# Third layer's remainders on GpSimd, seven-block one-hot batches of the pair stage on ScalarE, first layer's tail later in the step

## Chip, cores and metric

One core of one Trainium2 chip. The metric is the device time of one launch in microseconds, the slowest core's; here there is one. Engines: TensorE (PE), VectorE (DVE), ScalarE (ACT), GpSimd (POOL) and SyncE (SP, which only issues transfers). Lines as L777 are lines of the kernel before.

## What is computed

A graph of 6250 nodes with 64 features and 200000 random edges sorted by target goes through four layers, each with a residual and a layer norm:

```python
x = layernorm(x + sage(x))        # layer 1: mean over neighbours, two dense products (64->128->64), aggregated twice
x = layernorm(x + gcn(x))         # layer 2: 1/sqrt(deg) on both ends
x = layernorm(x + signed(x))      # layer 3
x = layernorm(x + attention(x))   # layer 4: softmax over the edges of a target

# layer 3
Wh  = h @ W + b;  Wr = Wh[row];  Wc = Wh[col]
sim = (Wr * Wc).sum(-1) / maximum(|Wr| * |Wc|, 1e-8)
base = adj_v * softplus(deg_coeff[0] * deg_v + deg_coeff[1]) * (row != col)
prop_pos = segment_sum(base *  relu( sim) * Wc, row)
prop_neg = segment_sum(base * -relu(-sim) * Wc, row)
out = scale * (coeff[0] * prop_pos + coeff[1] * prop_neg + coeff[2] * Wh)
```

## The kernel before

The nodes make 49 blocks of 128 (`NB`, `P`). The edges are grouped by pair of blocks: for source block i and target block j the slots of the pair hold up to 128 edges, one on each partition. Gathers and scatters become matmuls with one-hot matrices of 128x128 (slot against node within the block), built on the chip. Values for such matmuls are split in three bf16 parts (a value, its remainder, the remainder's remainder) so that they are exact enough.

The program is written by hand for each engine, with semaphores; each engine runs its instructions in the order in which they stand. It has a head (to about 190 us), the **pair stage** (to 1370), the second layer (to 1877), the **third layer** (to about 2900) and the fourth.

**Pair stage** (`pairs_*`, L473 to L840). A loop over `t`, each step in 13 sub-steps `n`, works on five blocks at once. For block j = t: edge records come in and are turned on TensorE (L582), VectorE marks the source blocks (L735), TensorE counts runs (offsets L593, `runs` L608 to L611), VectorE takes the ranks from them (`ranks`, L740). For j - 1: one-hots of ranks and fields on VectorE (L749, L754) and 108 slot matmuls on TensorE (L626), which put the edges in their slots (`E3`, L760, L763 and ScalarE's L555). For i = t - 3, all 49 pairs of a block: VectorE builds the one-hots of sources `OS` and targets `OD` in seven batches b of seven blocks (`hots`, L777, 14 instructions of 128x896); SP stores both for the later layers (L476, L477); TensorE multiplies `OS` with `OD` four blocks at a time into one of two PSUM buffers (`count`, L638), ScalarE evacuates (L542), and TensorE uses the counts against the node features (`use`, L651). The one-hots have three buffers (`NHB`); a batch waits for the count and the store of the batch three before. For d = t - 4 the first layer's dense part is run (`dense`): VectorE's sum and `cat` (L785 to L794), a transpose on TensorE (L663), two products (L666, L669) with ScalarE's evacuations between (L516, L521), ScalarE's `T` (L524, sub-step 9), VectorE's sum into `X` (L797, L800; sub-steps 9 and 10), a transpose of two rows of `E3` on TensorE (L674, L675; sub-step 10), and ScalarE's evacuation of it with two DMA issues (L529 to L532; sub-step 11).

**Third layer** (`pairs3_*`, L1108 to L1333). A loop over n, seven pairs (`G`) a step, 343 steps (`NG`). For step n + 4 the "columns" are built, one-hots of 128x1792 in place of loaded rows: every third step on ScalarE as Abs and Relu (L1211, L1213), else on VectorE (L1263). TensorE gathers both ends (L1171, L1178), ScalarE evacuates one (L1221), VectorE forms dot products (L1271, L1274, L1276) and after seven steps the coefficient of a block (L1282 to L1296). For step n - 8 the gathered rows are scaled: three blocks of seven (`KA`) on ScalarE (L1230), four on GpSimd (L1148). For n - 9 the first remainder is taken, three blocks on VectorE (`remainder`, L1300), four on GpSimd (L1153). For n - 10 GpSimd takes the second (L1158), and for n - 11 TensorE adds all up in the target block (`spread`, L1190). The values have four buffers.

Of the kernel before, what the change touches and what calls it, by code (L numbers as in the profile page):

```python
# [53 lines left out]
def gnn_kernel(nc, x, src, dst, eattr, ew, ew2, W1n, b1n, W1r, Wl1, bl1, W2n, b2n, W2r, Wl2, bl2,  # L54
               W2g, b2g, dcoef, cpar, spar, W3, watt, bias3, out):
    with ExitStack() as ctx:
# [256 lines left out]
        def head_dve(dve):  # L313
# [177 lines left out]
        def pairs_act(act):  # L491
# [14 lines left out]
            def dense(i, n):  # L506
# [18 lines left out]
                elif n == 11:  # L525
# [49 lines left out]
        def pairs_pe(pe):  # L575
# [79 lines left out]
            def dense(i, n):  # L655
# [14 lines left out]
                elif n == 10:  # L670
                    pe.wait_ge(t_out.at, i + 1)
# [35 lines left out]
        def pairs_dve(dve):  # L707
# [58 lines left out]
            def hots(i, n):  # L766
# [9 lines left out]
                for o_, s in ((OS, 0), (OD, 1)) if n == 0 else (((OS, 0),) if n % 2 else ((OD, 1),)):  # L776
                    ins = dve.tensor_tensor(o_[r].rearrange("p c (r k) -> p c r k", k=2), bc(r1v.unsqueeze(1), [P, 7, D, 2]),  # L777
                                            bc(sdb[i % 2][:, s, 7 * b:7 * b + 7, :].unsqueeze(2), [P, 7, D, 2]), ALU.is_equal)
                    (dv if s == 0 else hot8).by(ins)
# [426 lines left out]
        def pairs3_act(act):  # L1206
            def columns(n):
                if n % 3 == 0:
# [4 lines left out]
                    hot_a.by(act.activation(rw[r], rw[r], ACT.Relu, bias=1.0, scale=-1.0))  # L1213
# [44 lines left out]
        def pairs3_dve(dve):  # L1258
            def columns(n):
                if n % 3:  # L1260
# [17 lines left out]
            def coefficient(j):  # L1278
# [1027 lines left out]
```

## Time and profile before

| | us |
|---|---|
| median of 3 runs | 3884.51 (3882.99 to 3885.42) |
| profiled run | 3884.62 |
| its span, first to last instruction | 3882.9 |

| engine | busy us of the span | share |
|---|---|---|
| VectorE | 3187.8 | 82% |
| TensorE matmul | 3024.9 | 78% |
| ScalarE | 2164.4 | 56% |
| GpSimd | 1348.8 | 35% |

These shares are means over stages with different limits, so they say little alone; the stages are read one by one from busy times in a stretch of the span, then from the waits in it and from one step in order of time. A row of the order of time has start, length, engine, line and what is written from what; "x3" merges three instructions in a row, and the bracket is the idle time of the engine before it and what ended it. The clock granted to TensorE was 0.924 of its full speed on the mean.

### The profile page before, as it was taken

What the parts mean: (1) busy time and instruction counts of PE and PEld (TensorE: products, weight loads), DVE (VectorE), ACT (ScalarE), POOL (GpSimd) and SP (SyncE); (2) the same over time, 40 slices, a digit from 0 to 9 for tenths busy, and PEclk for the clock granted to TensorE, in tenths of its full rate; (3) what the DMA queues carried; (4) which work ended last, traced back from release to release, by engine and by line L of the source; (5) the groups of instructions that cost most, each with busy time, mean ns of one, the idle gap of its engine ahead of it and who ended that gap; (6) DMA issues with size and microseconds to landing.
All of it is one profiled execution on the core that took longest, in us unless ns stands there. A gap on an engine that the chain in (4) does not pass through costs nothing.

```text
span 3882.9 us, 125317 instructions
## 1 busy us (share of the span) xinstructions
PE 3024.9 (78%) x50473; PEld 2698.4 (69%) x50473; DVE 3187.8 (82%) x6939; ACT 2164.4 (56%) x5734; POOL 1348.8 (35%) x1644
## 2 busy tenths in 40 slices
PE   0288888888888869899777777777765888778876
PEld 0167777777777669899677777677755777777775
DVE  7599999999999823233799999999976889888886
ACT  5323333333333410001688788788765888888887
POOL 2000000000000000000487787787772555555554
PEclk9999999999999989999899999999986888888887
DMA  8156666666666779889677677677746888888884
GB/s 212 55 166 209 207 206 209 207 207 209 209 208 208 241 293 369 338 330 328 214 244 235 222 243 232 225 247 232 229 140 219 272 259 263 265 269 261 262 259 146
DMA packets 655937, 907.64 MB, mean 234 GB/s; under 512 B 363977, under 2 KB 587882, under 8 KB 636411
## 3 DMA queue, kind: packets, MB, share of 16 engines
q1 hardware_dynamic: 633240, 800.64, 64.1%
q10 hardware_dynamic: 19763, 94.38, 6.4%
q8 instruction: 406, 6.65, 0.7%
q0 software_dynamic: 2352, 4.52, 0.6%
q14 instruction: 176, 1.44, 0.1%
HBM read 651.96 MB, written 247.40 MB: 232 GB/s over the span
## 4 chain that ended last, share of the span: by engine, by line
DVE 38%; PE 32%; DMA 11%; ACT 9%; issue 8%; SPq 2%; POOL 1%; ACTq 0%; DVEq 0%; POOLq 0%
PE ps L626 8%; PE ps L964 7%; DVE U L754 5%; DMA U<-AD 3%; DMA A<-ROWS 3%; DVE EDG L777 3%; DMA T<-ROWS 3%; DVE U L1271 3%; DVE EDG L1300 3%; DVE U L1263 2%; PE ps L1178 2%; PE ps L1190 2%; PE ps L1171 2%; DVE U L1634 2%; SPq L1398 2%
## 5 line engine op out<-in xcount | busy, mean ns | idle before, releaser
L542 ACT ACTIVATE U<-ps 128x512 bf16<-128x512 f32 (+1 forms) x637 | 359.1, 573 | 666.1 <-PE ps L638 665.9
L1148 POOL TENSOR_TENSOR EDG<-U,edge 128x256 f32<-128x256 f32 x343 | 244.0, 711 | 850.8 <-DVE edge L1296 732.4
L1466 ACT ACTIVATE U<-U,T 128x65 f32<-128x65 f32 x1806 | 459.9, 340 | 86.0 <-PE ps L1554 81.4
L1178 PE MATMUL ps<-U 128*128 128x65 bf16 x7203 | 300.1, 198 | 217.7 <-DVE edge L1274 215.0
L487 POOL DMA_INDIRECT U<-REC,nod x49 | 48.8, 996 | 1160.7 <-PE ps L582 1038.5
L964 PE MATMUL ps<-U 128*128 128x192 bf16 x4802 | 416.5, 247 | 38.4 <-DVE U L1041 19.3
L964 PEld LDWEIGHTS ps<-U 128*128 128x128 bf16 x4802 | 401.6, 98 | 46.8 <-DMA U<-AD 24.2
L1178 PEld LDWEIGHTS ps<-U 128*128 128x128 bf16 x7203 | 261.2, 101 | 241.3 <-DVE edge L1274 237.4
L777 DVE TENSOR_TENSOR EDG<-edge,EDG 128x896 bf16<-128x896 bf16 x686 | 408.3, 621 | 10.0 <-DMA OSD<-EDG 9.0
L1492 POOL TENSOR_TENSOR U<-U 128x455 f32<-128x455 f32 x258 | 276.2, 1071 | 305.6 <-DVE U L1634 305.6
L651 PE MATMUL ps<-EDG,U 128*128 128x193 bf16 x2401 | 312.8, 252 | 62.0 <-ACT U L542 40.4
L626 PE MATMUL ps<-U 128*128 128x98 bf16 (+1 forms) x5292 | 341.9, 223 | 0.3 <-DVE U L754 0.3
L1158 POOL TENSOR_TENSOR EDG<-EDG 128x448 f32<-128x448 f32 x343 | 329.3, 960 | 25.0 <-DVE EDG L1300 25.0
L626 PEld LDWEIGHTS ps<-U 128*128 128x128 bf16 x5292 | 328.3, 98 | 5.3 <-DVE U L754 0.8
L1171 PE MATMUL ps<-U 128*128 128x65 bf16 x7203 | 298.7, 197 | 13.3 <-ACT U L1213 7.7
L754 DVE TENSOR_TENSOR U<-U 128x882 bf16<-128x882 bf16 x528 | 295.8, 616 | 0.0
L1171 PEld LDWEIGHTS ps<-U 128*128 128x128 bf16 x7203 | 280.8, 100 | 20.1 <-issue 12.6
L1230 ACT ACTIVATE EDG<-U,edge 128x64 f32<-128x64 f32 x1029 | 279.6, 338 | 19.1 <-DVE edge L1296 10.4
L1046 DVE TENSOR_REDUCE A<-ps 128x64 f32<-128x192 f32 x98 | 34.3, 355 | 293.8 <-PE ps L964 293.6
L651 PEld LDWEIGHTS ps<-EDG,U 128*128 128x128 bf16 x2401 | 181.4, 99 | 131.7 <-ACT U L542 120.1
L638 PE MATMUL ps<-EDG 128*128 128x128 bf16 x2401 | 245.6, 222 | 30.8 <-DVE EDG L777 30.8
L1221 ACT ACTIVATE U<-ps 128x455 f32<-128x455 f32 x343 | 185.1, 540 | 148.6 <-PE ps L1171 146.4
(302 smaller groups left out, 7328.1 us busy)
## 6 DMA issues: line engine op xcount, KB each, us to landing
U<-AD SPq DMA_DIRECT2D x98, 1568.0 KB, 8.7
U<-ROWS SPq DMA_DIRECT2D x343, 448.0 KB, 4.4
OND<-EDG SPq DMA_DIRECT2D x343, 224.0 KB
OSD<-EDG SPq DMA_DIRECT2D x343, 224.0 KB
AD<-U ACTq DMA_DIRECT2D x49, 1568.0 KB, 6.4
EDG<-ROWS SPq DMA_DIRECT2D x343, 224.0 KB, 5.1
U<-OND SPq DMA_DIRECT2D x303, 224.0 KB, 5.3
EDG<-OSD SPq DMA_DIRECT2D x189, 224.0 KB, 4.6
```

The costliest lines, as they stand in the source:

```text
L542: ev4.by(act.activation(prow[i % NPW][:, P * g:P * (g + m)], ps[4 + gg % 2][:, 0:P * m], ACT.Copy))
L626: ins = pe.matmul(ps[3][:, o:o + NB * (f1 - f0)], w_, FR[h][:, c, f0:f1, :, k], start=(h + c + k + f0 == 0), stop=(last and f0 == 0))
L651: ins = pe.matmul(ps[6][:, 0:XW], prow[i % NPW][:, P * j:P * j + P], Xs[:, j, :], start=(j == 0), stop=(j == NB - 1))
L754: ins = dve.tensor_tensor(FR[h][:, :, f, :, :], OH[j % 2][:, HC * h:HC * h + HC, :, :], bc(L_[j % NL][:, 2 + f, HC * h:HC * h + HC, :].uns ...
L777: ins = dve.tensor_tensor(o_[r].rearrange("p c (r k) -> p c r k", k=2), bc(r1v.unsqueeze(1), [P, 7, D, 2]), bc(sdb[i % 2][:, s, 7 * b:7 * ...
L964: ins = pe.matmul(ps[q][:, 0:192], arow[r][:, P * j:P * j + P], (XsB if p else XsA)[:, j, :, :].rearrange("p s f -> p (s f)"), start=(j == ...
L1158: low3.by(pool.tensor_tensor(V3[m % 4][:, 2, :, :], V3[m % 4][:, 1, :, :], S3[m % 4][:, 1, :, :], ALU.subtract))
L1171: ins = pe.matmul(ps[h][:, 65 * k:65 * k + 65], rw[r][:, 2 * P * k + P:2 * P * k + 2 * P], Ws[:, i0 + k, s_, 0:65], start=(s_ == 0), stop= ...
L1178: ins = pe.matmul(ps[2 + h][:, 65 * k:65 * k + 65], rw[r][:, 2 * P * k:2 * P * k + P], Ws[:, j, s_, 0:65], start=(s_ == 0), stop=(s_ == 2))
L1230: ins = act.activation(V3[m % 4][:, 0, k, :], Wc[:, j % 2, i0 + k, 0:D], ACT.Copy, scale=edge[:, 6 + j % 2, i0 + k:i0 + k + 1])
L1466: ins = act.activation(V4[k % NV][:, 0, c, :], H[d % 3][:, s, :], ACT.Copy, scale=a4[d % 2][:, s:s + 1])
L1492: look.by(pool.tensor_tensor(V4[k % NV][:, 2, :, :], V4[k % NV][:, 1, :, :], S4[k % NV][:, 1, :, :], ALU.subtract))
```

## The change

1. Third layer: the first remainder of all seven blocks is GpSimd's, which waits for ScalarE's copies; VectorE's `remainder` is gone. `KA` is 5 instead of 3, so ScalarE scales five blocks and GpSimd two. ScalarE builds the columns of every fifth step instead of every third, VectorE the others. The coefficient is one instruction shorter, from a constant `sc[:, 19:20]` made in the head.
2. Pair stage: the targets' one-hots `OD` of batches 2 and 5 are made by ScalarE (`hots` in `pairs_act`), as Abs of a difference per block and one Relu per batch, spread over sub-steps 0 to 4 and 5 to 9; SP and TensorE wait for them on a semaphore of their own. There are four buffers instead of three, the fourth in `U`.
3. First layer's tail: VectorE's two sums go from sub-steps 9 and 10 to 11 and 12, TensorE's row transposes from 10 to 12 (and no longer wait for `T`), ScalarE's evacuation of them from 11 to 12.

The diff, cut to its core:

```diff
-        NHB = 3
+        NHB = 4
+        BYA = (2, 5)
...
 def pairs_sp
                 sp.wait_ge(hot8.at, k + 1)
+                if b in BYA:
+                    sp.wait_ge(hot_a.at, hot_a.o + made_a(k))
...
 def pairs_act, dense
-                elif n == 11:
+                elif n == 12:
                     act.wait_ge(row_t.at, i + 1)
...
+            def hots(i, n):
+                if n >= 5 * len(BYA):
+                    return
+                b = BYA[n // 5]
+                k = NH7 * i + b
+                r = k % NHB
+                if n % 5 == 0:
+                    act.wait_ge(slot_ev.at, i + 1)
+                    if k >= NHB:
+                        kk = k - NHB
+                        act.wait_ge(count4.at, NG4 * (kk // NH7) + (7 * (kk % NH7) + 6) // 4 + 1)
+                        act.wait_ge(hot_st[r].at, 32 * (k // NHB))
+                for c in ((0, 1), (2, 3), (4, 5), (6,), ())[n % 5]:
+                    ac.by(act.activation(OD[r][:, c, :], iota1, ACT.Abs, scale=-1.0, bias=E3[:, i, 1, 7 * b + c:7 * b + c + 1]))
+                if n % 5 == 4:
+                    act.wait_ge(ac.at, ac.n)
+                    hot_a.by(act.activation(OD[r].rearrange("p c r -> p (c r)"), OD[r].rearrange("p c r -> p (c r)"), ACT.Relu, bias=1.0, scale=-1.0))
...
                     if d is not None:
                         dense(d, n)
+                    if i is not None:
+                        hots(i, n)
...
 def pairs_pe
+                pe.wait_ge(hot_a.at, hot_a.o + made_a(NH7 * i + (g + m - 1) // 7))
...
-                elif n == 10:
-                    pe.wait_ge(t_out.at, i + 1)
+                elif n == 12:
                     pe.wait_ge(x_in.at, i + 1)
...
 def pairs_dve, dense
-                elif n == 9:
+                elif n == 11:
                     dve.wait_ge(t_out.at, i + 1)
...
-                elif n == 10:
+                elif n == 12:
                     dve.wait_ge(x_in.at, i + 1)
...
 third layer
-        KA = 3
+        KA = 5
...
-            return n // 3 + 1
+            return n // 5 + 1
...
                     pool.wait_ge(vm_p.at, m + 1)
-                    rem3p.by(pool.tensor_tensor(V3[m % 4][:, 1, KA:G, :], V3[m % 4][:, 0, KA:G, :], S3[m % 4][:, 0, KA:G, :], ALU.subtract))
+                    pool.wait_ge(vm_a.at, m + 1)
+                    rem3.by(pool.tensor_tensor(V3[m % 4][:, 1, :, :], V3[m % 4][:, 0, :, :], S3[m % 4][:, 0, :, :], ALU.subtract))
...
-                if n % 3 == 0:
+                if n % 5 == 0:
...
-                dvf.by(dve.tensor_scalar(a, b_, 0.0, sc[:, 16:17], ALU.max, ALU.mult))
-                dvf.by(dve.tensor_scalar(c_, b_, 0.0, sc[:, 17:18], ALU.min, ALU.mult))
+                dvf.by(dve.tensor_scalar(a, b_, 0.0, sc[:, 19:20], ALU.max, ALU.mult))
                 dve.wait_ge(dvf.at, dvf.n)
-                dvf.by(dve.tensor_tensor(a, a, c_, ALU.add))
+                dvf.by(dve.scalar_tensor_tensor(a, b_, sc[:, 17:18], a, ALU.mult, ALU.add))
```

VectorE in the pair stage around the sum into `X`, sub-steps 9 to 12, before (L777 is a one-hot batch):

```order
L754 TENSOR_TENSOR U<-U,EDG 128x9x98 x2
L797 TENSOR_TENSOR X<-X,ps 128x64 [waits t_out]
L777 TENSOR_TENSOR EDG<-edge,EDG 128x896 [waits hot_st2,pair_count,slot_evac]
L800 TENSOR_TENSOR X<-X,brow 128x64 [waits x_in]
L777 TENSOR_TENSOR EDG<-edge,EDG 128x896
```

and in the change, where the numbers of lines have moved (L815 is a batch of `OS`, L819 one of `OD`, L838 and L841 are L797 and L800):

```order
L792 TENSOR_TENSOR U<-U,EDG 128x9x98 x2
L815 TENSOR_TENSOR EDG<-edge,EDG 128x896 [waits hot_st0,pair_count,slot_evac]
L838 TENSOR_TENSOR X<-X,ps 128x64 [waits t_out]
L815 TENSOR_TENSOR EDG<-edge,EDG 128x896 [waits hot_st1,pair_count,slot_evac]
L841 TENSOR_TENSOR X<-X,brow 128x64 [waits x_in]
L819 TENSOR_TENSOR EDG<-edge,EDG 128x896
```

The sum stands one batch later, and the batch of `OD` between is gone.

ScalarE in the pair stage from sub-step 7 on, before (L542 evacuates counts, L521 the hidden layer, L504 the turned records, L524 writes `T`, L529 the rows):

```order
L521 ACTIVATE MISC<-ps,bias1s 128x128 [waits layer_out,hidden]
L504 ACTIVATE U<-ps 128x360 [waits field_hot,rec_turned]
L542 ACTIVATE U<-ps 128x512 [waits pair_count] x2
L524 ACTIVATE T<-ps 128x64 [waits layer_out]
L542 ACTIVATE U<-ps 128x512 [waits pair_count] x2
L529 ACTIVATE EDG<-ps 49x256 [waits rw_st0,rows_t]
L531 DMA ROWS<-EDG 49x256 [waits rows_ev]
L532 DMA ROWS<-EDG 49x2x128
```

and in the change (L578 Abs, L581 Relu, L559 evacuation, L538, L521, L541, L546 for L521, L504, L524, L529):

```order
L538 ACTIVATE MISC<-ps,bias1s 128x128 [waits layer_out,hidden]
L578 ACTIVATE EDG<-edge,E 128x128 x2
L521 ACTIVATE U<-ps 128x360 [waits field_hot,rec_turned]
L559 ACTIVATE U<-ps 128x512 [waits pair_count]
L578 ACTIVATE EDG<-edge,E 128x128
L559 ACTIVATE U<-ps 128x512 [waits pair_count]
L541 ACTIVATE T<-ps 128x64 [waits layer_out]
L581 ACTIVATE EDG<-EDG 128x896 [waits act_step]
L559 ACTIVATE U<-ps 128x512 [waits pair_count] x3
L546 ACTIVATE EDG<-ps 49x256 [waits rw_st0,rows_t]
L548 DMA ROWS<-EDG 49x256 [waits rows_ev]
L549 DMA ROWS<-EDG 49x2x128
```

Three Abs and a Relu stand between the evacuations, and the row evacuation with its two issues comes after one more evacuation of counts.

VectorE in the third layer, one step, before:

```order
L1271 TENSOR_TENSOR U<-ps,U 128x448 [waits r_got,c_ev]
L1274 TENSOR_TENSOR edge<-ps,U 128x7 [waits coef]
L1276 TENSOR_REDUCE edge<-U 128x7 [waits fast_step]
L1263 TENSOR_SCALAR U<-U,iotap 128x1792 [waits rows_ld4]
L1300 TENSOR_TENSOR EDG<-EDG 128x192 [waits value_act]
```

and GpSimd's and VectorE's work in the change (GpSimd's is L1185 for L1148, L1191 for L1153, L1195 for L1158):

```order
L1185 TENSOR_TENSOR EDG<-U,edge 128x128 [waits spread,coef]
L1191 TENSOR_TENSOR EDG<-EDG 128x448 [waits value_act,value_pool]
L1195 TENSOR_TENSOR EDG<-EDG 128x448 [waits layer_out]
...
L1308 TENSOR_TENSOR U<-ps,U 128x448 [waits r_got,c_ev]
L1311 TENSOR_TENSOR edge<-ps,U 128x7 [waits coef]
L1313 TENSOR_REDUCE edge<-U 128x7 [waits fast_step]
L1300 TENSOR_SCALAR U<-U,iotap 128x1792 [waits rows_ld4]
```

VectorE has no operation on the values any more, and GpSimd's remainder of all 448 columns waits for ScalarE's copies.

## Rows read from the trace of the kernel before

**Rows 1.** Busy time by stretch: pair stage and third layer.

```profile
core 0: us, PE busy (x) PEld busy (x) DVE busy (x) ACT busy (x) POOL busy (x), PEclk, DMA share, GB/s
300.00:1300.00 1000.00, 885.85 (x11893) 717.51 (x11891) 971.12 (x1963) 362.70 (x873) 35.68 (x39) 1.00 0.67 209
1900.00:2800.00 900.00, 686.95 (x15045) 648.70 (x15041) 860.65 (x1882) 725.02 (x1515) 703.59 (x915) 0.94 0.72 236
```

**Rows 2.** Waits, 200 to 1300 us: total us, times, longest us.

```profile
DVE X L797 <- ACT T L524: 27.9, 44, 0.7
```

**Rows 3.** One step in order of time: start us, us, engine, line [idle <-releaser].

```profile
1004.81 0.34 PE L611 MATMUL ps<-EDG,identb 18*128 18x98 bf16 x4
...
1005.75 1.13 DVE L740 TENSOR_REDUCE EDG<-ps 128x10 bf16<-128x490 f32 x2
...
1005.89 0.41 PE L638 MATMUL ps<-EDG 128*128 128x128 bf16 x4 [0.40 <-DVE EDG L777]
...
1008.15 0.33 PE L663 MATMUL ps<-ident,MISC 128*128 128x128 f32 x1 [0.66 <-DVE MISC L794]
...
1016.54 0.36 ACT L521 ACTIVATE MISC<-ps,bias1s 128x128 f32<-128x128 f32 x1
...
1016.79 0.47 ACT L504 ACTIVATE U<-ps 128x360 bf16<-128x360 bf16 x1
...
1017.80 0.28 PEld L651 LDWEIGHTS ps<-EDG,U 128*128 128x128 bf16 x4 [0.28 <-ACT U L542]
...
1018.48 0.22 DVE L797 TENSOR_TENSOR X<-X,ps 128x64 f32<-128x64 f32 x1 [0.63 <-ACT T L524]
1018.62 0.62 DVE L777 TENSOR_TENSOR EDG<-edge,EDG 128x896 bf16<-128x896 bf16 x1
...
1019.29 1.69 DVE L777 TENSOR_TENSOR EDG<-edge,EDG 128x896 bf16<-128x896 bf16 x3
...
1023.14 0.36 ACT L529 ACTIVATE EDG<-ps 49x256 bf16<-49x256 f32 x1
...
1024.23 1.08 ACT L542 ACTIVATE U<-ps 128x512 bf16<-128x512 f32 x2 [0.72 <-PE ps L638]
...
1026.00 1.10 PE L593 MATMUL ps<-U,after 128*18 128x49 bf16 x36
...
1029.71 0.66 DVE L740 TENSOR_REDUCE EDG<-ps 128x10 bf16<-128x490 f32 x1
```

**Rows 4.** Groups by line, VectorE, third layer: xcount | busy us, mean ns | idle.

```profile
L1300 DVE TENSOR_TENSOR EDG<-EDG 128x192 f32<-128x192 f32 x305 | 192.3, 631 | 18.7 <-ACT EDG L1230 17.9
...
L1263 DVE TENSOR_SCALAR U<-U,iotap 128x1792 bf16<-128x1792 bf16 x204 | 177.2, 869 | 0.0
```

**Rows 5.** The same of ScalarE.

```profile
L1230 ACT ACTIVATE EDG<-U,edge 128x64 f32<-128x64 f32 x918 | 249.5, 338 | 5.5 <-DVE edge L1296 5.3
L1211 ACT ACTIVATE U<-U,negp 128x1792 bf16<-128x1792 bf16 x102 | 181.3, 1777 | 0.0
L1213 ACT ACTIVATE U<-U 128x1792 bf16<-128x1792 bf16 x102 | 173.1, 1697 | 3.2
L1221 ACT ACTIVATE U<-ps 128x455 f32<-128x455 f32 x306 | 165.3, 540 | 134.5 <-PE ps L1171 132.5 <-POOL EDG L1148 0.9
```

**Rows 6.** Single lines, third layer: duration ns min/median/max.

```profile
L1148 POOL TENSOR_TENSOR EDG<-U,edge x305: 605/638/1109, 1900.0 to 2799.4; 128x256 f32<-128x256 f32 x153
...
L1158 POOL TENSOR_TENSOR EDG<-EDG x305: 924/928/1365, 1899.1 to 2798.5; 128x448 f32<-128x448 f32 x153
...
L1263 DVE TENSOR_SCALAR U<-U,iotap x204: 676/741/1392, 1900.1 to 2796.7; 128x1792 bf16<-128x1792 bf16 x102
...
L1300 DVE TENSOR_TENSOR EDG<-EDG x305: 344/702/1102, 1901.7 to 2797.3; 128x192 f32<-128x192 f32 x153
```

**Rows 7.** In order of time, third layer, VectorE beside GpSimd.

```profile
2309.97 0.61 POOL L1148 TENSOR_TENSOR EDG<-U,edge 128x256 f32<-128x256 f32 x1
...
2310.32 0.75 DVE L1263 TENSOR_SCALAR U<-U,iotap 128x1792 bf16<-128x1792 bf16 x1
```

More of the change, by code:

```diff
@@ L434, in gnn_kernel @@
         Xs3 = Xs[:, :, 0:3 * D].rearrange("p b (s f) -> p b s f", s=3)
-        NHB = 3
+        NHB = 4
         NH7, GH = 7, 7 * P
-        OS = [EDG[:, 4730 + 448 * i:4730 + 448 * i + 448].bitcast(BF16).rearrange("p (c r) -> p c r", r=P) for i in range(NHB)]
-        OD = [EDG[:, 6074 + 448 * i:6074 + 448 * i + 448].bitcast(BF16).rearrange("p (c r) -> p c r", r=P) for i in range(NHB)]
+        spare = part(o2 + 6272, 896)
+        OS = [o.bitcast(BF16).rearrange("p (c r) -> p c r", r=P)
+              for o in [EDG[:, 4730 + 448 * i:4730 + 448 * i + 448] for i in range(NHB - 1)] + [spare[:, 0:448]]]
+        OD = [o.bitcast(BF16).rearrange("p (c r) -> p c r", r=P)
+              for o in [EDG[:, 6074 + 448 * i:6074 + 448 * i + 448] for i in range(NHB - 1)] + [spare[:, 448:896]]]
+        BYA = (2, 5)
         rst = [EDG[:, 7802 + P * i:7802 + P * i + P].bitcast(BF16) for i in range(2)]
@@ L466, in gnn_kernel, with made_a @@
         hot_st = [sem(f"hot_st{i}") for i in range(NHB)]
+        def made_a(k):
+            return len(BYA) * (k // NH7) + sum(b <= k % NH7 for b in BYA)
         def at_step(t):
@@ L775, in hots @@
                         dve.wait_ge(hot_st[r].at, 32 * (k // NHB))
[L776 to L779, printed above, removed]
+                if n % 2 or n == 0:
+                    ins = dve.tensor_tensor(OS[r].rearrange("p c (r k) -> p c r k", k=2), bc(r1v.unsqueeze(1), [P, 7, D, 2]),
+                                            bc(sdb[i % 2][:, 0, 7 * b:7 * b + 7, :].unsqueeze(2), [P, 7, D, 2]), ALU.is_equal)
+                    (hot8 if b in BYA else dv).by(ins)
+                if n % 2 == 0 and b not in BYA:
+                    hot8.by(dve.tensor_tensor(OD[r].rearrange("p c (r k) -> p c r k", k=2), bc(r1v.unsqueeze(1), [P, 7, D, 2]),
+                                              bc(sdb[i % 2][:, 1, 7 * b:7 * b + 7, :].unsqueeze(2), [P, 7, D, 2]), ALU.is_equal))
             def dense(i, n):
@@ L1212, in columns @@
                     act.wait_ge(ac.at, ac.n)
-                    hot_a.by(act.activation(rw[r], rw[r], ACT.Relu, bias=1.0, scale=-1.0))
+                    hot_ea.by(act.activation(rw[r], rw[r], ACT.Relu, bias=1.0, scale=-1.0))
             def ends(n):
@@ L1296, in coefficient @@
                 coef.by(dve.tensor_tensor(d_, a, E3v[:, :, j, 2], ALU.mult))
-            def remainder(m):
-                dve.wait_ge(vm_a.at, m + 1)
-                rem3.by(dve.tensor_tensor(V3[m % 4][:, 1, 0:KA, :], V3[m % 4][:, 0, 0:KA, :], S3[m % 4][:, 0, 0:KA, :], ALU.subtract))
             for n in range(4):
@@ L1304, in pairs3_dve @@
             for n in range(NLAST):
-                if 0 <= n - 9 < NG:
-                    remainder(n - 9)
                 if n < NG:
@@ L1713, in gnn_kernel @@
         z_inc, z_carry, z_fix, z_agg, z_read = again(ln_i), again(ln_o), again(normed), again(pj_t), again(pj_ev)
-        z_cat, z_t, z_ct, z_h, z_r, z_o, z_x2 = again(pj_mm), again(pj_out), again(nr_i), again(nr_o), again(ws_i), again(ws_o), again(hot_a)
+        z_cat, z_t, z_ct, z_h, z_r, z_o, z_x2 = again(pj_mm), again(pj_out), again(nr_i), again(nr_o), again(ws_i), again(ws_o), again(hot_ea)
         z_tab, z_tabst = again(hot_d), again(c_got)
```

18 lines of the change are left out of this document (10 added, 8 removed).

## Prediction

> **What bounds the kernel now.** I read first the busy time by stretch, because the page's shares mix stages. In the pair stage (300 to 1300 us taken) VectorE is busy 97.1% of the time and TensorE 88.6%; ScalarE has only 36%. In the third layer (1900 to 2800 us taken) VectorE is busy 95.6%, ScalarE 80.6%, GpSimd 78.2%, TensorE 76.3% [rows 1]. So VectorE is the engine to relieve in both, and the change does that. What matters is who is second.
>
> The waits of the pair stage come next [rows 2]. VectorE waits for one thing, `T` from ScalarE, 0.63 us a step. Then I read one step in order of time [rows 3]: TensorE in turn waits there for VectorE, 0.40 us for a one-hot batch and 0.66 for `cat` (L794), so the two hold each other. It lasts 1029.71 - 1005.75 = 23.96 us from one start of L740 to the next. TensorE's last run-count matmuls (L611) end at 1004.81 + 0.34 = 1005.15; VectorE starts the ranks that need them (L740) only at 1005.75, so it is late there by about 0.5. From that start, ranks, fields and `cat` take 2.35 us, and TensorE, which waited for `cat`, goes on at 1008.15. From 1008.15 to the next 1005.15 + 23.96 TensorE never again waits for VectorE, only for ScalarE. **This is the number that decides the pair stage**: VectorE can give back about 0.5 us a step before TensorE's own loop, which runs through ScalarE's evacuations, sets the pace.
>
> In the third layer a step of seven blocks lasts 900 / 305 = 2.95 us [rows 1, 4] (305 is the count of L1300 in that stretch). By the same division VectorE is busy 2.82 us of it, ScalarE 2.38, GpSimd 2.31, TensorE 2.25. VectorE has no room here, and its remainder (L1300) has a mean of 631 ns where its minimum is 344 [rows 4, 6].
>
> **Pair stage, part by part.**
> - VectorE loses two of fourteen one-hots. Three in a row take 1.69 where one takes 0.62 [rows 3], so one costs 0.535 from start to start: 2 x 0.535 = 1.07 us a step. Its wait of 0.63 for `T` would be a further gain if it vanished.
> - TensorE's gain. With VectorE early, the ranks start just behind the run counts, 1005.23 for 1005.75, and `cat` comes 0.52 us earlier. **-0.52**. Without `cat` TensorE would be there at 1008.15 - 0.66 = 1007.49; two Abs ahead of an evacuation (0.54, below) put that later and the 0.40 of waiting for a one-hot batch, which goes, earlier: 1007.63, just when `cat` is there. So the whole 0.52 stands.
> - ScalarE's additions. Seven Abs of 128x128 and a Relu of 128x896 per batch, in pieces between the evacuations (the second order listing). A 128x128 activation with its bias from a tile takes 0.36, and the next starts 0.25 after it (1016.54, 1016.79) [rows 3]; for a source in SBUF I add 0.02, an estimate, and take 0.27. Where TensorE has much else to do these are hidden: before the first count group ScalarE sits idle, and after the third there are 5 us of run counts and slot matmuls. They show at one place, sub-step 7 to 9: between the copy of the records (L504, 1016.79) and what stands ahead of it (L521, 1016.54) two Abs are put, ahead of the evacuation for which TensorE already waits (0.28 us at 1017.80). **+0.55**, up to 0.8 if an Abs takes its full 0.36 and more. The Relu at sub-step 9 lies beside the 3.4 us of slot matmuls.
> - The tail moved later. The row transposes and ScalarE's row evacuation with two DMA issues stood at sub-steps 10 and 11, now both at 12. Today the row evacuation starts at 1023.14 and the next count evacuation 1.09 us later, at 1024.23, and TensorE waits for it [rows 3]. In the new order the transposes come behind one more count and one more use group, so the evacuation starts at about 1023.9, the same 1.09 us then delay the next group (1024.99 + 0.60), and only the last two use groups (0.6 us) follow: the next step starts at about 1026.25 for 1026.00. **+0.25**.
> - VectorE's wait for `T` does not go. Today VectorE is there at 1018.48 - 0.63 = 1017.85. It comes there 0.52 earlier with its whole step, and batch 5's second one-hot (-0.54) is gone while its first now stands ahead (+0.54): 1017.33. `T` comes 0.52 earlier and three Abs later (+0.8): 1018.76. It waits about 1.45 us. It then still reaches the next ranks some 0.4 us before TensorE has ended the run counts, so the longer wait costs nothing.
> - The fourth buffer and the stores: SP now waits for ScalarE's mark at batches 2 and 5, and batch 6 and the next step's queue behind it. ScalarE's marks fall at sub-steps 4 and 9, as VectorE's did; the buffer is wanted again four batches later, over 6 us. I take nothing.
>
> Sum: -0.52 + 0.55 + 0.25 = +0.28 us in each of 48 full steps: **+13 us**. Ends: -0.52 alone if both additions hide (-25 us), and no gain at `cat` with +0.85 (+41 us).
>
> **Third layer, part by part**, per step of 2.95 us [rows 1, 4 to 6].
> - VectorE: the remainder goes, 0.631 less 0.085 of overlap = -0.55. Columns rise from 2/3 to 4/5 of the steps, 0.133 x (0.869 - 0.085) = +0.10. The coefficient has one small operation less in seven steps, -0.03 (the head has one more, once: nothing). New 2.34; if every column operation is held by GpSimd for another 0.15, 2.46.
> - GpSimd: scaling two blocks instead of four. The minima for 256 and 448 columns are 0.605 and 0.924, 1.66 ns a column, so -0.21; the remainder grows from 256 to 448 columns, +0.32. New 2.31 + 0.11 = 2.42. It no longer waits for VectorE's part (L1158) but for ScalarE's scaled copies.
> - ScalarE [rows 5]: two more copies, 2 x (0.338 - 0.10) = +0.48; columns fall from 1/3 to 1/5 of the steps, 0.133 x (1.777 + 1.697) = -0.46. New 2.40.
> - TensorE unchanged, about 2.25 with its short waits in it.
>
> So the bound falls from 2.82 to about 2.42, and three engines then lie within 0.1 of each other. Today the step is 1.045 of its busiest engine. With ScalarE's block of 3.5 us every fifth step, and waits in both directions between three full engines, I take 1.10: 2.67 us, **-0.28 us a step**. The steps with values are 343 - 9 = 334: **-94 us**. Ends: 2.52 (1.045 of 2.42), -144 us; and 2.85, -33 us, if the queues (four value buffers, two of PSUM) don't ride over the blocks.
>
> **A rule against it.** In the trace VectorE and GpSimd hold each other up: the column operation that starts at 2310.32 beside GpSimd's of 2309.97 (to 2310.58) takes 0.75 where the minimum is 0.676, and GpSimd's three operations (L1153 has the shape of L1148) have minima of 0.605 + 0.605 + 0.924 = 2.13, but are busy 2.31 [rows 1, 6, 7]. If all such operations exclude each other for their whole length, a step has 2.13 of GpSimd, 0.667 x 0.68 of columns and 0.34 of remainder: 2.93, nearly today's 2.95. After the change it would be 2.24 + 0.8 x 0.68 = 2.78, scaled by 2.95 / 2.93 to 2.80: -0.15 x 334 = -50 us. Against it: the column operation above was delayed by 0.07, though GpSimd's had 0.26 to go.
> The Trainium skill ("SBUF — State Buffer", section "Who interferes with whom") states it so: the shared port pair is held for the whole instruction and the loser fully blocks. By that the third layer gives 50 us rather than 94; the traced pair of operations speaks for a shorter hold.
>
> **The rivals.**
> 1. VectorE stays the bound of the pair stage: 1.07 + 0.63 = 1.70 us x 48 = -82, with -94 gives 3709 us. For it speaks its 97%; against it the 0.5 us of room above. 8%.
> 2. Whole-length exclusion between VectorE and GpSimd, as above: 3884.6 + 13 - 50 = 3848 us. 17%.
> 3. Slower: GpSimd's remainder waits for ScalarE's block. Between the last copies before a block and the next lie 3.47 of columns, 0.54 of evacuation and 0.34 + 4 x 0.24 of five copies, 5.3 us, against 2.42 of GpSimd's own work: 2.9 us per five steps, 0.58 a step, 3.00 in all, +0.05 x 334 = +17, and with the pair stage 3915 us. It decides this way if ScalarE enters a block with no lead over GpSimd; with 2.9 us of lead it costs nothing. Against it: VectorE's remainder has the same wait today and sits 17.9 us in it over 305 steps [rows 4], with blocks every third step. 7%.
>
> **Numbers.** The profiled run took 3884.6 us, 1.7 more than its span, and the median of three is 3884.5, so the sum needs no shift. Forecast: 3884.6 + 13 - 94 = **3804 us**, 62%. The remaining 6% are things not seen, split evenly. The range is 3742 to 3874: the ends of both stages taken together would be 3716 and 3893, and the range leaves out rival 1, rival 3 and the outermost of these. A measurement can tell 0.2%, about 8 us. Faster by more: 0.86; within: 0.07; slower: 0.07.
>
> **What would show it.** Pair stage: a step of 24.0 to 24.4 us, VectorE's busy share down to about 92% with a wait for ScalarE's `T` of 1 to 2 us a step and a new short wait for the run counts, ScalarE near 60%. A step under 23.4 us would break the argument on TensorE's loop. Third layer: steps of 2.5 to 2.85 us, GpSimd over 85% busy, VectorE under 92%. The column operation's mean above 0.95 us with GpSimd's operations stretched speaks for rival 2; GpSimd's 128x448 remainder waiting over 150 us for ScalarE's copies speaks for rival 3. The second and fourth layers should not move.

## The result, and the profile after

| | median, us | ratio to before, 95% interval |
|---|---|---|
| before | 3883.51 (3871.6 to 3887.23, 10 runs) | |
| changed | 3893.5 (3886.1 to 3910.43, 10 runs) | 1.0039 [1.0027, 1.0051] |

The changed kernel is slower by 0.4%, 10 us, where 3804 us and a gain of 2% were forecast; the time lies outside the range. The profiled run of the changed kernel took 3910.43 us and is the slowest of its ten, so the two traces differ by more (span 3908.7 for 3882.9, +25.8) than the medians do: what is read below from one trace is larger than what the ten executions have on the median. Ratios, here and below, are to the kernel before as it was measured together with the changed one.

Busy time in the stretches of [rows 1], same columns; the changed kernel:

```profile
300.00:1300.00 1000.00, 866.22 (x11437) 706.06 (x11435) 893.69 (x1803) 572.77 (x1482) 91.64 (x39) 0.96 0.63 201
1900.00:2800.00 900.00, 695.27 (x15232) 657.06 (x15233) 841.44 (x1613) 737.18 (x2024) 725.04 (x898) 0.92 0.74 241
```

VectorE has fallen from 97.1% to 89.4% in the pair stage, as meant, but PEclk from 1.00 to 0.96. In the third layer VectorE is still at 93.5% (95.6% before).

The third layer's first product in each of its steps marks that stage. Before, then changed (duration ns min/median/max, first and last start):

```profile
L1271 DVE TENSOR_TENSOR U<-ps,U x343: 609/611/625, 1881.2 to 2877.6; 128x448 f32<-128x448 f32 x172
```
```profile
L1308 DVE TENSOR_TENSOR U<-ps,U x343: 609/612/626, 1921.8 to 2893.0; 128x448 f32<-128x448 f32 x172
```

So of the 25.8 us the stages up to the third layer lost 40.6, the third layer gave back 996.4 - 971.2 = 25.2 (94 were forecast), and what lies behind it was 10.4 longer. Nothing is changed there, and it is scatter between executions: from the last of these products to the end it takes 998 to 1016 us in the 14 traces of this case. The third layer scatters too: with it as before it takes 992 to 996 us in four traces (this first one, `pair_alone`, `tail_alone` and `hots_alone`), and with part 1 962 to 974 in seven, so its gain is known to be 18 to 35 us and no closer.

**Pair stage.** I took the step from one start of VectorE's sum into `X` (L838 now, L797 before) to the next. Before, all of the 43 full steps (the last five are shorter) take 23.95 to 24.00 us. Now 30 take 24.1 to 24.4 (forecast: 24.24), and 13, every third or so, take 26.2 to 26.7. 13 x 2.06 = 27 us for these (26.42 for 24.36) and 43 x 0.34 = 15 for the normal growth give 42, and 40.6 of it are left where the third layer begins. The waits from 300 to 1300 us, of VectorE for `T` and for the run counts, to be held against [rows 2], and of TensorE for ScalarE's count evacuation (total us, times, longest us):

```profile
DVE X L838 <- ACT T L541: 68.1, 40, 2.5
DVE EDG L778 <- PE ps L649: 35.5, 40, 2.0
```
```profile
PE ps L690 <- ACT U L559: 103.8, 148, 1.6
```

1.70 us a step for `T` and the new wait for run counts (L649) are what was foretold. A long step from inside, in order of time and then by stretch (columns of [rows 1]), changed kernel:

```profile
1000.69 0.38 ACT L546 ACTIVATE EDG<-ps 49x256 bf16<-49x256 f32 x1
...
1001.40 0.57 ACTq L549 DMA_DIRECT2D ROWS<-EDG  x1
...
1002.01 0.77 ACT L559 ACTIVATE U<-ps 128x512 bf16<-128x512 f32 x2 [0.95 <-PE ps L677]
...
1002.67 0.60 PE L690 MATMUL ps<-EDG,U 128*128 128x193 bf16 x5 [1.32 <-ACT U L559]
...
1004.69 0.59 PE L646 MATMUL ps<-U,triub 128*128 128x490 bf16 x1 [0.39 <-ACT EDG L594]
```
```profile
1000.00:1004.60 4.60, 2.98 (x58) 2.42 (x56) 4.60 (x11) 1.97 (x6) 0.00 (x0) 1.00 0.82 251
1004.60:1011.80 7.20, 6.85 (x41) 3.79 (x41) 5.46 (x14) 4.75 (x14) 0.00 (x0) 0.53 0.64 234
1011.80:1024.00 12.20, 11.27 (x159) 10.18 (x158) 9.80 (x21) 6.41 (x17) 1.69 (x1) 1.00 0.46 132
```

The row evacuation (L546) and two DMA issues stand ahead of a count evacuation (L559), so TensorE waits 1.32 us at the use behind it; then for 7 us the granted clock is 0.53, close to the lower of its two levels (1.2 GHz of 2.4), and L646 takes 0.59 us, where the same matmul takes 0.38 at full clock (before, below). Then it is 1.00 again. The same place before:

```profile
1023.14 0.36 ACT L529 ACTIVATE EDG<-ps 49x256 bf16<-49x256 f32 x1
...
1024.88 0.51 PE L651 MATMUL ps<-EDG,U 128*128 128x193 bf16 x4 [0.83 <-ACT U L542]
...
1027.49 0.38 PE L608 MATMUL ps<-U,triub 128*128 128x490 bf16 x1 [0.39 <-ACT EDG L558]
```

TensorE's longest wait is this one, 0.82 us in nearly every step (1.02 to 1.28 in three), and the clock is 1.00 in all full steps. Each of the 13 long steps has one such stretch at the lower level, and no other step has one; that the clock is what costs the 2.06 us is tested in experiment 5.

**Third layer**, groups by line, 1900 to 2800 us (columns of [rows 4]; GpSimd's first):

```profile
L1195 POOL TENSOR_TENSOR EDG<-EDG 128x448 f32<-128x448 f32 x298 | 306.6, 1029 | 0.0
L1191 POOL TENSOR_TENSOR EDG<-EDG 128x448 f32<-128x448 f32 x299 | 292.9, 980 | 96.1 <-ACT EDG L1267 96.1
L1300 DVE TENSOR_SCALAR U<-U,iotap 128x1792 bf16<-128x1792 bf16 x249 | 261.3, 1050 | 0.0
...
L1332 DVE TENSOR_TENSOR edge<-edge,E 128x49 f32<-128x49 f32 x44 | 29.7, 674 | 1.5
```

The column operation is 1050 ns for 869, and the coefficient's last (L1332 now, L1296 before) 674 for 246. What happens to them, in order of time, changed kernel:

```profile
2309.30 0.93 POOL L1191 TENSOR_TENSOR EDG<-EDG 128x448 f32<-128x448 f32 x1
2309.55 0.74 DVE L1323 TENSOR_TENSOR edge<-edge 128x49 f32<-128x49 f32 x1
2310.19 0.93 POOL L1195 TENSOR_TENSOR EDG<-EDG 128x448 f32<-128x448 f32 x1
2310.32 0.83 DVE L1325 TENSOR_SCALAR edge<-edge,sc 128x49 f32<-128x49 f32 x1
...
2311.43 0.93 POOL L1191 TENSOR_TENSOR EDG<-EDG 128x448 f32<-128x448 f32 x1
2311.57 0.90 DVE L1332 TENSOR_TENSOR edge<-edge,E 128x49 f32<-128x49 f32 x1
```

Each of VectorE's three, of 0.21 to 0.25 us at their shortest, begins behind one of GpSimd's and ends just behind its end: 2310.29 behind 2310.23, 2311.15 behind 2311.12, 2312.47 behind 2312.36. VectorE sits out the rest of GpSimd's operation. The column operations show it without an exception: of the 274 of the changed kernel 186 last over 0.70 us, and each of these ends 0.47 to 0.50 us behind an end of GpSimd's; the other 88 take 0.68. Before, it was 154 of 228, with the same 0.48. Operations with one input from PSUM (L1308, 0.61) and reductions (L1313, 0.62) keep their length beside GpSimd. The Trainium skill ("SBUF — State Buffer", section "Who interferes with whom") says which: VectorE's tensor operations with two SBUF inputs, and copies and tensor-scalar ones in two-port modes, share a port pair with GpSimd under an exclusive lock, while reductions don't. The rows agree for the tensor operations, the tensor-scalar ones and the reductions; they have no copy of this kind.

### The profile page after: what moved, and what is told of

Same layout as the page of the kernel before. It is cut to its first block, busy times and chain, and to the rows that moved or that the text cites. A ratio compares the mean times of both kernels' runs of the same rounds, so it can differ in the third digit from the quotient of the medians.

```text
span 3908.7 us, 126442 instructions
## 1 busy us (share of the span) xinstructions
PE 3045.4 (78%) x50473; PEld 2719.7 (70%) x50473; DVE 3097.7 (79%) x6496; ACT 2445.7 (63%) x7112; POOL 1443.9 (37%) x1644
## 4 chain that ended last, share of the span: by engine, by line
PE 37%; DVE 26%; ACT 13%; DMA 10%; issue 8%; SPq 2%; POOL 2%; ACTq 1%; DVEq 0%; POOLq 0%
PE ps L664 8%; PE ps L1005 7%; ACT U L559 4%; PE ps L690 4%; DVE U L1300 4%; DMA U<-AD 3%; DVE U L1308 3%; DMA T<-ROWS 3%; DMA A<-ROWS 3%; PE ps L677 2%; DVE U L1664 2%; SPq L1428 2%; PE ps L649 2%; PE ps L646 2%; DVE EDG L1669 2%
## 5 line engine op out<-in xcount | busy, mean ns | idle before, releaser
L559 ACT ACTIVATE U<-ps 128x512 bf16<-128x512 f32 (+1 forms) x637 | 357.3, 571 | 428.3 <-PE ps L677 425.4
L504 POOL DMA_INDIRECT U<-REC,nod x49 | 106.2, 2167 | 1141.7 <-PE ps L620 1019.8
L1267 ACT ACTIVATE EDG<-U,edge 128x64 f32<-128x64 f32 x1715 | 443.6, 338 | 8.2 <-PE ps L1227 5.9
L1185 POOL TENSOR_TENSOR EDG<-U,edge 128x128 f32<-128x128 f32 x343 | 173.8, 507 | 708.3 <-DVE edge L1332 675.6
L1191 POOL TENSOR_TENSOR EDG<-EDG 128x448 f32<-128x448 f32 x343 | 336.1, 980 | 108.8 <-ACT EDG L1267 108.7
L1195 POOL TENSOR_TENSOR EDG<-EDG 128x448 f32<-128x448 f32 x343 | 351.0, 1024 | 0.0
L1208 PEld LDWEIGHTS ps<-U 128*128 128x128 bf16 x7203 | 282.2, 101 | 20.9 <-issue 10.7
L1300 DVE TENSOR_SCALAR U<-U,iotap 128x1792 bf16<-128x1792 bf16 x274 | 287.8, 1051 | 0.0
```

What stands on the lines that cost most here:

```text
L559: ev4.by(act.activation(prow[i % NPW][:, P * g:P * (g + m)], ps[4 + gg % 2][:, 0:P * m], ACT.Copy))
L1191: rem3.by(pool.tensor_tensor(V3[m % 4][:, 1, :, :], V3[m % 4][:, 0, :, :], S3[m % 4][:, 0, :, :], ALU.subtract))
L1195: low3.by(pool.tensor_tensor(V3[m % 4][:, 2, :, :], V3[m % 4][:, 1, :, :], S3[m % 4][:, 1, :, :], ALU.subtract))
L1208: ins = pe.matmul(ps[h][:, 65 * k:65 * k + 65], rw[r][:, 2 * P * k + P:2 * P * k + 2 * P], Ws[:, i0 + k, s_, 0:65], start=(s_ == 0), stop= ...
L1267: ins = act.activation(V3[m % 4][:, 0, k, :], Wc[:, j % 2, i0 + k, 0:D], ACT.Copy, scale=edge[:, 6 + j % 2, i0 + k:i0 + k + 1])
L1300: hot_d.by(dve.tensor_scalar(rw[r], rw[r], iotap[:, 0:1], None, ALU.is_equal))
```

## Experiments

**1 to 4: the parts alone.** Part 1 is the third layer's, 2 the one-hots on ScalarE, 3 the later tail. `pair_alone` is parts 2 and 3 on the kernel before, `third_alone` part 1, `tail_alone` part 3, `hots_alone` part 2; each takes its hunks of the diff shown above and no other line. In the table, "6 of 26.4" stands for six long steps among the 43.

> Parts 2 and 3 of the change (ScalarE's one-hots, four buffers, tail later), third layer as before. If the pair stage's loss is its own (last one-hot at 1405 us for 1362), the whole 42 us come here: about 3925 us, +1.1%, with the third layer's step back at 2.95 us. If part of the loss were the third layer's start, it would be less than 25 us.

> Part 1 alone. If the third layer's gain is independent, its stage is 25 us shorter and the time about 3858 us (-0.65%), VectorE still over 94% busy there with columns at 1.07 us. The rival, that the stage gained only because it started in another phase behind the pair stage, expects under 10 us.

> Part 3 alone: all one-hots on VectorE. Working of the prediction: VectorE's wait of 0.63 us for T goes almost whole, TensorE's loop grows by 0.25 of its 0.5 us of room: steps of about 23.7 us, -13 us in all, granted clock 1.0. Rival: the tail is what makes TensorE idle long enough for its clock to fall: steps of 24.3 and more with clock under 0.98, +15 to +40 us.

> Part 2 alone: ScalarE's one-hots and four buffers, tail where it was. If the Abs between the evacuations carry the cost: steps of 24.0 to 24.3 us, 0 to +15 us in all, wait for T about 2 us a step on VectorE. If the fall of TensorE's clock belongs to ScalarE's extra work and not to the tail, granted clock 0.97 or less in 300 to 1300 us and +30 us or more.

| kernel | us | ratio, 95% interval | first third-layer product, us | pair-stage steps, us |
|---|---|---|---|---|
| before | | | 1881.2 | 23.96 |
| `third_alone` | 3855.56 | 0.995 [0.9933, 0.9967] | 1879.4 | as before |
| `pair_alone` | 3918.03 | 1.0103 [1.0079, 1.0127] | 1913.6 | 24.35, 6 of 26.4 |
| `tail_alone` | 3868.87 | 0.9975 [0.9962, 0.9988] | 1865.2 | 23.56, 2 of 25.3 and 25.7 |
| `hots_alone` | 3893.63 | 1.0043 [1.003, 1.0056] | 1891.9 | 24.19 |

The two parts of the pair stage moved the first product by -16.0 and +10.7 us alone and by +32.4 together: the difference of some 38 is neither's own. Over the 43 full steps it is 29 us, the rest comes up behind them. Some 20 of the 29 are the normal step, on the mean 24.31 where 23.97 - 0.36 + 0.24 = 23.85 would stand if the parts added up, and 9 are long steps. That 0.46 is about the 0.52 by which VectorE comes late to the ranks before: each part alone makes up for most of that, and it can be had only once. This account is worked out from the four traces; no run tests it by itself. `tail_alone` fits it: VectorE's wait for `T` vanished (0.5 us in all), VectorE now waits for the run counts, and the step is 0.40 shorter. So by this account the later tail itself costs TensorE some 0.12 us (0.52 less 0.40), where +0.25 stood. The waits of VectorE for run counts, 200 to 1300 us, in `tail_alone` and in `one_only` (below, one batch on ScalarE instead of two):

```profile
DVE EDG L739 <- PE ps L611: 15.4, 44, 2.4
```
```profile
DVE EDG L778 <- PE ps L649: 29.9, 44, 2.0
```

In `hots_alone` VectorE has no such wait. It waits 1.95 us a step for `T` (forecast: 1.45) and begins the ranks some 0.25 us behind the run counts, so there part of the 0.52 wasn't gained. All four came within 7 us of what was expected, and the steps too but for `tail_alone`'s 23.56 (23.7). `third_alone` shortened its stage by 34.6 us, with the column operation at 1085 ns (1950 to 2750 us).

**5: the clock.** `filler` is the changed kernel with TensorE kept busy where it waited:

```diff
                     count(i, NG4 - 1)
+                    if j is not None:
+                        pe.wait_ge(rank_ok.at, 2 * j + 2)
+                        for _ in range(16):
+                            pe.matmul(ps[0][:, 0:P], onesb[:, :], iota2[:, 0:P], start=True, stop=True)
                     use(i, NG4 - 2)
```

> The changed kernel with 16 extra 128x128 matmuls on TensorE, into a buffer nobody reads, at the place where it waits 1.3 us for the last count evacuations. If its clock falls in every third step because it sat idle there, the falls go: granted clock 1.0 in 300 to 1300 us, all steps 24.1 to 24.5 us, pair stage about 25 us shorter, 3868 us. If the falls come from something else (the first wait for the offsets, the transfers), the clock stays at 0.96 and the time within 8 us of the changed kernel.

3877.09 us, ratio 0.9986 [0.9974, 0.9998], where the changed kernel has 1.0039 [1.0027, 1.0051]; the first product at 1900.2 for 1921.8, every full step 24.1 to 24.9. The pair stage by stretch, and the filler (L742) with the use behind it:

```profile
300.00:1300.00 1000.00, 892.51 (x12380) 744.96 (x12378) 915.39 (x1851) 586.25 (x1518) 103.66 (x39) 1.00 0.65 205
```
```profile
402.81 1.06 PE L742 MATMUL ps<-iota,onesb 128*128 128x128 bf16 x16
404.30 0.60 PE L690 MATMUL ps<-EDG,U 128*128 128x193 bf16 x5 [0.43 <-ACT U L559]
```

Added work whose result nobody reads takes 26.1 us off the 43 steps (21.6 at the first product), the clock is back at 1.00, and no stretch at the lower level is left. So the 27 us of long steps are the clock's, and here idle time of TensorE brings its fall on. Of the +19 us left against before, 43 x 0.37 = 16 are the longer normal step (24.34 on the mean).

**6 and 7: the wait itself.** `rows_last` puts the row evacuation and its issues behind the step's last count evacuations, `one_batch` moreover leaves batch 5 with VectorE:

```diff
-                    if d is not None:
+                    if d is not None and n != NG4 - 1:
                         dense(d, n)
...
                     count(i, NG4 - 1)
+                if d is not None:
+                    dense(d, NG4 - 1)
```
```diff
-        BYA = (2, 5)
+        BYA = (2,)
```

> The changed kernel with ScalarE's row evacuation and its two issues behind the last two count evacuations of the step. By TensorE's loop: the wait of 1.3 us shrinks to under 0.4, the step is 24.3 - 1.0 = 23.3 us, and no falls of the clock: -27 and -48 us, about 3820 us. If VectorE's wait for T carries the step instead (T at ScalarE's sub-step 9, then 10.2 us of VectorE's work to the next ranks), steps stay at 23.9 or more: 3845 us or more.

> rows_last with only batch 2 on ScalarE (batch 5 back on VectorE). No Abs stand between the evacuations of sub-steps 5 to 9. TensorE's loop 23.96 - 0.52 - 1.0 = 22.5, VectorE's work 23.96 - 0.63 - 0.54 = 22.8: steps of about 22.9 us, -56 us against the kernel before in the pair stage, 3800 us with the third layer's gain. If the order of the evacuations is not what holds TensorE, no better than rows_last.

Both missed. `rows_last`: 3910.22 us, 1.0063 [1.0039, 1.0087], PEclk 0.92. The wait only moved, in order of time:

```profile
608.18 0.38 ACT L546 ACTIVATE EDG<-ps 49x256 bf16<-49x256 f32 x1 [0.76 <-ACT U L559]
608.59 0.27 ACTq L548 DMA_DIRECT2D ROWS<-EDG  x1
608.89 1.24 ACTq L549 DMA_DIRECT2D ROWS<-EDG  x1
610.17 0.29 ACT L594 ACTIVATE EDG<-ps,sc 18x49 bf16<-18x49 f32 x1 [1.61 <-issue]
...
610.52 0.38 PE L648 MATMUL ps<-U,triub 128*128 128x490 bf16 x1 [1.58 <-ACT EDG L594]
```

The issues now stand ahead of the offsets' evacuation (L594), and TensorE waits 1.58 us for that, 1.35 in most steps; 19 of the 43 steps are over 25.2 us. `one_batch`: 3867.68 us, 0.997 [0.9955, 0.9984]; its steps alternate between 23.6 and 24.2 with four above 26, PEclk 0.95, and TensorE waits 1.30 for the offsets. I had forgotten the next step's first consumer of ScalarE.

**8: contention in the third layer.** `less_pool` is `third_alone` with one of seven blocks of GpSimd's second remainder; it leaves out the other six, whose third part keeps old values:

```diff
-low3.by(pool.tensor_tensor(V3[m % 4][:, 2, :, :], V3[m % 4][:, 1, :, :], S3[m % 4][:, 1, :, :], ALU.subtract))
+low3.by(pool.tensor_tensor(V3[m % 4][:, 2, 0:1, :], V3[m % 4][:, 1, 0:1, :], S3[m % 4][:, 1, 0:1, :], ALU.subtract))
```

> third_alone with GpSimd's second remainder taken over one block of seven instead of seven (the third part of the other values is left stale): GpSimd's busy share falls from 0.85 to about 0.6. If GpSimd's operations lengthen VectorE's (mean 1.07 us for the columns, 0.5 to 0.7 for the coefficient's small ones), these fall towards 0.75 and 0.25 to 0.4 us and the step from 2.80 towards 2.55, 60 to 85 us less than third_alone. If the columns are slow for another reason (the transfers into the same buffers), they stay above 1.0 us and the time within 15 us.

3777.1 us, 0.9726 [0.9707, 0.9745]; the stage takes 893.2 us for the 961.8 of `third_alone`. Groups by line, 1950 to 2750 us, `third_alone` and then `less_pool`:

```profile
L1265 DVE TENSOR_SCALAR U<-U,iotap 128x1792 bf16<-128x1792 bf16 x226 | 245.2, 1085 | 0.0
...
L1297 DVE TENSOR_TENSOR edge<-edge,E 128x49 f32<-128x49 f32 x40 | 24.0, 601 | 1.4
```
```profile
L1156 POOL TENSOR_TENSOR EDG<-EDG 128x448 f32<-128x448 f32 x304 | 325.0, 1069 | 174.3 <-ACT EDG L1232 168.7 <-POOL EDG L1150 0.4
...
L1265 DVE TENSOR_SCALAR U<-U,iotap 128x1792 bf16<-128x1792 bf16 x242 | 190.8, 788 | 0.0
...
L1160 POOL TENSOR_TENSOR EDG<-EDG 128x64 f32<-128x64 f32 x303 | 110.6, 365 | 0.0
...
L1297 DVE TENSOR_TENSOR edge<-edge,E 128x49 f32<-128x49 f32 x43 | 14.6, 340 | 1.6 <-DVE edge L1292 0.2
```

VectorE's work is the same, and GpSimd's second remainder falls from 1038 to 365 ns; the column operation falls by 297 ns, 0.8 x 0.30 = 0.24 us a step, and the stage by 68.6 / 342 = 0.20 us a step. GpSimd had idle time all along (it waited 84.9 us in 800 for ScalarE in `third_alone`), so I take it that the gain came through VectorE. That the shorter chain of GpSimd's operations helped by itself isn't excluded by this run alone; but in `ka6` below GpSimd has less work too, and the step grows.

**9 to 12: toward a better version.** `tail_third` is parts 1 and 3. `ka6` is that with `KA = 6`, and `ka6_seven` has besides the three tests `n % 5` and `n // 5` of the third layer's columns as `n % 7` and `n // 7`. `one_only` is the changed kernel with `BYA = (2,)`.

> Parts 1 and 3 of the change together, all targets' one-hots left on VectorE. My theory: the two parts touch different stages and don't meet, so their gains add: 15 us for the later tail and 28 us for the third layer taken alone on their medians, some 25 on the stage in this case's noise: 3842 us (3835 to 3855). Pair stage: steps of 23.56 us with the clock at 1.00 and no step of 26.4. Third layer: steps of 2.82 to 2.88 us, column operation near 1.08 us. Rival: the pair stage's better state is itself fragile (the clock falls in some executions, as with part 2), then 3860 to 3870 and steps of over 25 us in it.

> The kernel of parts 1 and 3 with one more of the seven blocks scaled by ScalarE (KA = 6), so that GpSimd scales one. Theory of contention: what counts in the third layer is how long GpSimd holds VectorE up. Taking 0.67 us a step from GpSimd gave 0.23 us a step; here its operation falls from 0.51 to about 0.36 us, so 0.05 us a step, 17 us: some 3825 us, with the column operation's mean near 1.04. Rival: with 2.42 + 0.24 = 2.66 us of work and blocks of 3.5 us in between ScalarE now makes GpSimd wait longer (today 0.30 us a step), and the step stays or grows: 3842 to 3860 us, the 128x448 remainder waiting over 130 us in 900 for ScalarE.

> The changed kernel with one batch of seven (batch 2) of the targets' one-hots on ScalarE, batch 5 back on VectorE. Theory: TensorE's clock falls where its wait at the first use group grows to 1.3 us; the two Abs of batch 5 at sub-steps 7 to 9 and the later start of ScalarE's row evacuation make it so, and batch 2's pieces stand where ScalarE is idle. Without batch 5 the steps are 23.6 to 23.9 us, none or few of 26.4, and the first product of the third layer comes near 1870 us: 3850 to 3862 us. Rival: any batch on ScalarE is enough to tip it: several steps above 26 us and 3870 us or more.

> The kernel with KA = 6 and the later tail, with ScalarE building the columns of every seventh step instead of every fifth. If the loss of KA = 6 alone came from ScalarE's column blocks of 3.5 us holding GpSimd's remainder up, fewer blocks give it back: ScalarE has 0.057 x 3.48 = 0.20 us a step less, VectorE 0.057 x 1.0 = 0.06 more, GpSimd keeps the shorter scaling. Steps of 2.78 to 2.84 us where KA = 5 had 2.88, GpSimd's wait for ScalarE's copies back at 90 to 110 us in 800: 3815 to 3840 us. Rival: VectorE, at 95% with KA = 5, takes the extra columns badly, 2.88 us or more: 3845 to 3860 us.

| kernel | us | ratio, 95% interval | third layer, us | GpSimd waits for ScalarE's copies, 1950 to 2750 |
|---|---|---|---|---|
| `tail_third` | 3844.53 | 0.9906 [0.9892, 0.992] | 972.3 | 88.6 |
| `ka6` | 3869.31 | 0.9971 [0.9959, 0.9983] | 992.0 | 137.7 |
| `ka6_seven` | 3836.52 | 0.9893 [0.9875, 0.9912] | 965.3 | 116.9 |
| `one_only` | 3846.48 | 0.9903 [0.9886, 0.992] | 964.5 | 80.6 |

The parts without the one-hots on ScalarE give 1% over the kernel before. `tail_third` has three steps of 25.3 to 25.6 us, where none was expected, `ka6` two and `ka6_seven` none. One batch on ScalarE costs nothing and gains nothing: VectorE is at 96.1% in its pair stage, and the steps are 23.6 with three of 25.6 to 25.9. Against the changed kernel `one_only` differs by batch 5 alone, and its first product comes at 1874.7 us for 1921.8. So batch 5 on ScalarE costs 47 us: 0.7 us in each normal step (24.30 for 23.59), and ten of the 13 long ones. `ka6` went the way of its rival, ScalarE's blocks hold GpSimd up, though it came out above the rival's range of 3842 to 3860 us; with blocks every seventh step the loss is gone. `ka6_seven` and `tail_third` can't be told apart by their intervals.

## Why the prediction was wrong

Two steps failed: VectorE's load in the third layer was too small, and the granted clock was not in the sum. Of the 106 us between the forecast and the traced execution 69 are the first's, 28 the pair stage's (41 for 13, nearly all of it the clock's 27) and 10 scatter behind the third layer.

- **Pair stage, normal step: right in the sum.** 24.24 us forecast, 24.30 found on the mean. By the account above the terms nearly fit too: -0.52 is gained once, the later tail costs 0.12 where +0.25 stood, and batch 5 costs 0.7 where +0.55 stood ("up to 0.8"). 23.96 - 0.52 + 0.12 + 0.7 = 24.3; the two misses cancelled in part. That TensorE's loop and not VectorE decides held in the changed kernel, where VectorE waits 0.89 us a step for run counts, and in `tail_alone` and `one_only`; no full step of any run fell under 23.4. It did not hold in `hots_alone`, where VectorE's wait for `T` made it late. The forecast counted 48 full steps; there are 43.
- **The clock: not in the sum.** I treated each wait of TensorE at its own length, and none of the rivals had the granted clock in it, though [rows 1] had the column with 1.00. It cost 27 us. That the stage lost just the 41 us of my upper end ("no gain at `cat` with +0.85") is chance: that way of losing them did not occur. The two pessimistic ends together gave 3893, the measured median, and the range left them out.
- **Third layer, ScalarE and GpSimd: right.** ScalarE 737.18 / 309 = 2.39 us a step (2.40 forecast), GpSimd 0.510 + 0.980 + 1.029 = 2.52 (2.42).
- **Third layer, VectorE: the failed step**, "New 2.34; if every column operation is held by GpSimd for another 0.15, 2.46". It is 841.44 / 309 = 2.72. So the bound did not fall "from 2.82 to about 2.42", GpSimd's, but to VectorE's 2.72, and 971.2 / 342 = 2.84 us is the step. The column operations grew by 0.18, and by growing in number too they cost +0.24 in place of +0.10. The small operations were taken at their old length: L1332 went from 246 to 674 ns, and with its neighbours they add some 0.2 us a step to the forecast. VectorE's remainder is gone, but GpSimd is now busy in longer pieces, and VectorE's other operations run into them. Without most of one of those pieces (`less_pool`) VectorE has 712.40 / 303 = 2.35 us. That is near the forecast of 2.34, but it does not confirm it: GpSimd's load there is 539.10 / 303 = 1.78 and not 2.42, so a GpSimd of 2.42 beside a VectorE of 2.34 was never run.
- **The rule I set aside was right.** Rival 2 had 17% and gave -50 us for the stage; it was -25 (-35 with part 1 alone). I held the pair of [rows 7] against it: the column operation was only 0.07 late. Read again: GpSimd's ends at 2310.58, and VectorE's at 2311.07, 0.49 later. In the changed kernel, in order of time, it is the same:

```profile
2302.13 0.93 POOL L1191 TENSOR_TENSOR EDG<-EDG 128x448 f32<-128x448 f32 x1
2302.42 1.12 DVE L1300 TENSOR_SCALAR U<-U,iotap 128x1792 bf16<-128x1792 bf16 x1
```

  The column operation ends at 2303.54, 0.48 behind GpSimd's end of 2303.06, as every lengthened one does. So of its 0.676 us only the first 0.19 runs beside GpSimd's, and the rest waits to the end. I had taken the start-up for an overlap. The rival itself fell short because it, too, left the small operations out.
- **Rival 3** did not decide: GpSimd's remainder waited 96.1 us in 900, under the 150 named, though in `ka6`, with more copies, this mechanism did cost 20 us.
- The second layer is unmoved: 507 us from the last sum into `X` to the first product, for 510 before.

What stays open: which idle time makes the clock fall. Before and with part 2 alone TensorE's longest wait for ScalarE is 0.82 us in nearly every step, and the clock is 1.00 in all full steps. In the four kernels with the later tail and no one-hots on ScalarE it is 1.10, in `one_only` 1.13, and none to three of 43 steps are long. With both parts it is 1.32, and 6 (`pair_alone`) or 13 (changed) are. Longer waits go with more falls, but the length of one wait doesn't decide: 1.32 is followed by a fall in some steps and by none in others, one of 1.61 in `pair_alone` by none, and one of 1.09 in the changed kernel by one. `pair_alone` and the changed kernel have the same instructions in this loop and were traced once each, so the number of falls probably changes between executions as well.

## To carry over

Where VectorE and GpSimd share a stage, count for each of VectorE's operations with two SBUF inputs or in a two-port mode the rest of GpSimd's operation that it may run into; work moved from one to the other frees little, and long operations on GpSimd hurt VectorE's shortest ones most. When a change hands idle time to TensorE, look at the granted clock of the stretches behind it: the price can be slower matmuls there, and not only the wait. When two edits touch one loop, price them together: both may free the same wait, which can be gained only once (0.5 us a step here), and together they brought falls of the clock that neither had often alone; their sum here was off by 38 us.

## What the hardware showed

- A wait of mostly 1.32 us was followed in 13 of 43 steps by about 7 us at a granted clock of 0.53 and 2.06 us of lost time; 16 matmuls whose result nobody reads, 1.06 us in all, put in the wait, undid it.
- An operation of VectorE of 0.25 us (L1332) lasted 0.90 beside GpSimd's of 0.93. A column operation of 0.68 us that met one of GpSimd's ended 0.48 us behind it in all 186 cases of the changed kernel and all 154 before, so 0.19 us of start-up overlap and no more.
- ScalarE's two DMA issues hold its next evacuation up. The second of them took 0.34 us on the median before, 0.57 in the changed kernel (L549), and 1.29 where it stood behind the step's last count evacuation (`rows_last`); why it differs is open.
